# A new order of all steps and fewer idle TensorE products in a single-core hybrid block

## The reference

```
x = x + attention(layernorm(x))   # 16 heads of 8, causal window of 32 plus every 64th key
x = x + ffn(layernorm(x))         # 128 -> 512 -> 512 -> 128, weights +1/-1, relu
x = x + mamba(layernorm(x))       # which itself returns its input plus its output
x = x + ffn(layernorm(x))         # the same ffn again
```

```
h[t] = exp(dt[t] * A) * h[t-1] + (dt[t] * u[t]) * B[t]
y[t] = sum over n of h[t] * C[t]
```

## Time and profile before

| | |
|---|---|
| median of three timed executions | 776.4 us (775.49, 776.4, 776.85) |
| the profiled execution | 773.7 us |
| its span | 771.9 us |
| around the span | 1.8 us |
| mean granted TensorE clock | 0.996 of full speed |

### The profile page before, as it was taken

One profiled execution on the slowest core, in us unless ns is written; L12 is line 12 of the kernel. 1 busy time (PEld: TensorE's weight loads), 2 busy tenths in 40 slices (PEclk: granted clock), 3 DMA queues, 4 the chain that ended last, 5 costly groups with the idle time before them and its releaser, 6 DMA issues. The chain is left out here.

```text
span 771.9 us, 21849 instructions
## 1 busy us (share of the span) xinstructions
PE 710.7 (92%) x8031; PEld 403.9 (52%) x8031; DVE 685.3 (89%) x1138; ACT 640.6 (83%) x1282; POOL 610.4 (79%) x599
## 2 busy tenths in 40 slices
PE   7889999998999989999999999979998999888798
PEld 4676644644555346547555356445464453343356
DVE  6988339989999999999999899999999999899973
ACT  4778688999989999998889999988979866856633
POOL 5013347888998999788898789999999999999960
PEclk9999999999999999999999999999999999999989
DMA  6000014533524161423425171525261525254410
GB/s 211 3 3 2 3 46 152 164 97 107 186 71 138 45 200 63 135 77 107 128 64 183 46 232 58 178 92 174 69 192 46 178 83 178 91 171 144 143 42 28
DMA packets 45003, 83.56 MB, mean 108 GB/s; under 512 B 5081, under 2 KB 5730, under 8 KB 44898
## 3 DMA queue, kind: packets, MB, share of 16 engines
q1 hardware_dynamic: 44898, 82.18, 33.5%
HBM read 71.15 MB, written 11.01 MB: 106 GB/s over the span
## 5 line engine op out<-in xcount | busy, mean ns | idle before, releaser
L1820 POOL TENSOR_TENSOR d<-d,cr 128x1024 f32<-128x1024 f32 x128 | 300.1, 2355 | 17.4 <-DVE d L1315 6.9
L1632 ACT ACTIVATE ps<-dt,An 128x512 f32<-128x512 f32 x252 | 172.2, 696 | 36.7 <-DVE d L1315 36.0
L1315 DVE TENSOR_TENSOR_SCAN d<-ps,hl,d 128x512 f32<-128x512 f32 x128 | 157.2, 1262 | 5.0 <-ACT ps L1632 4.3
L1315 DVE TENSOR_TENSOR_SCAN d<-ps,d 128x512 f32<-128x512 f32 x128 | 149.9, 1205 | 7.2 <-ACT ps L1632 6.9
L886 PE MATMUL ps<-h,w 128*128 128x512 f16 (+1 forms) x512 | 115.8, 379 | 6.6 <-DVE h L1243 6.3
L1303 DVE TENSOR_TENSOR d<-ps,du 128x512 f32<-128x512 f32 x173 | 111.6, 671 | 3.8 <-ACT ps L1615 2.2
L1806 POOL TENSOR_TENSOR d<-du,br 128x512 f32<-128x512 f32 x79 | 99.9, 1276 | 5.7 <-PE ps L981 4.1
L886 PEld LDWEIGHTS ps<-h,w 128*128 128x128 f16 x512 | 48.1, 99 | 76.1 <-DVE h L1243 17.8
L981 PE MATMUL ps<-d,cst 128*32 128x512 f32 x512 | 68.1, 604 | 3.2 <-POOL d L1820 3.2
L897 PEld LDWEIGHTS ps<-w,h 128*128 128x128 f32 x496 | 58.2, 192 | 8.3 <-issue 5.5
L897 PE MATMUL ps<-w,h 128*128 128x128 f32 x496 | 60.6, 277 | 0.8 <-ACT h L1529 0.8
(11 more groups left out here) (186 smaller groups left out, 1373.0 us busy)
## 6 DMA issues: line engine op xcount, KB each, us to landing
cr<-bcd SPq DMA_DIRECT2D x64, 256.0 KB, 3.3
br<-bcd SPq DMA_DIRECT2D x64, 256.0 KB, 3.1
dt<-dtd SPq DMA_DIRECT2D x64, 256.0 KB, 3.9
du<-dud SPq DMA_DIRECT2D x64, 256.0 KB, 3.6
dtd<-sR SPq DMA_DIRECT2D x16, 256.0 KB, 3.0
dud<-sE SPq DMA_DIRECT2D x16, 256.0 KB, 2.3
X<-in_x SPq DMA_DIRECT2D x8, 256.0 KB, 6.4
out<-X SPq DMA_DIRECT2D x3, 512.0 KB, 4.0
```

What stands on the lines that cost most here:

```text
L1315: eng.tensor_tensor_scan(d, banks[u % NG][:, :], d, hl[:, r:r + 1] if m % 2 else 0.0, ALU.mult, ALU.add).then_inc(v_sc, 1)
L1632: eng.activation(banks[u % NG][:, :], src[:, :], ACT.Exp, scale=An[:, g:g + 1]).then_inc(s_da, 1)
L1820: eng.tensor_tensor(d, d, CR[k % NC][:, :].unsqueeze(1).to_broadcast((128, n, 512)), ALU.mult).then_inc(p_cm, n)
```

## The change

Three things change; no instruction outside the idle products is added or removed, and which engine runs a tile's drive stays.

1. All numbers of `PLACES` are new. Compared as orders, 648 of ScalarE's 946 steps stand at another position, 453 of VectorE's 798, 312 of TensorE's 704, 158 of GpSimd's 322 and 230 of the DMA queue's 302. Most move by a few positions; the furthest are `jexp_s(1, 1)` (34 earlier), `aln_p(3, 0)` (40 later), `afar_v(1, 3)` (25 later).
2. `WARM` holds 33 runs with 173 `warm_t` products in place of 32 runs with 207 (the first entry, 8 products of `wake_t`, stays). With numbers over 570,000 stand 106 products in place of 139; of these, with numbers from 690,000 to 730,000, 28 in place of 28.
3. `bdt_t` loses a wait.

```
-    "gate_p": [172166, 214728, 261005, 292325, 372528, 374202, 429085, 457150, 499682, 548281, 574574, 607798, 665247, 680832, 715753],
...
+    "gate_p": [170696, 213613, 247300, 284326, 370996, 373530, 442779, 456599, 514580, 539318, 572679, 603283, 678895, 680122, 721855],
...
-    "silu_s": [100306, 167620, 255442, 322000, 426697, 483530, 573445, 645357],
...
+    "silu_s": [100445, 166698, 254325, 321662, 424921, 483026, 571576, 643475],
...
 WARM = [
-    (8848, 2, 8), (10191, 0, 3), (16231, 2, 8), (21682, 0, 6), (23005, 1, 3), (34876, 3, 2), (111358, 6, 8), (129053, 2, 5),
-    (206279, 7, 4), (263399, 4, 5), (265231, 4, 3), (436700, 7, 8), (457969, 2, 4), (495463, 2, 9), (574181, 7, 4), (585926, 7, 6),
-    (609134, 4, 6), (612224, 4, 4), (614591, 2, 4), (630052, 5, 6), (634479, 5, 14), (647873, 6, 9), (655387, 5, 12), (662679, 5, 15),
-    (679413, 4, 2), (682168, 4, 9), (687207, 5, 12), (690266, 6, 8), (695529, 6, 2), (711634, 7, 9), (714721, 6, 9), (739706, 4, 4), (741039, 5, 4),
+    (8675, 2, 8), (10186, 0, 3), (14787, 3, 4), (20658, 0, 3), (21937, 1, 3), (23263, 2, 3), (29410, 5, 2), (30734, 5, 3), (32013, 6, 1),
+    (34871, 3, 6), (48143, 7, 1), (50796, 3, 4), (127930, 2, 7), (263916, 4, 3), (266254, 6, 5), (269065, 5, 4), (455392, 2, 6),
+    (485725, 6, 6), (497891, 7, 3), (581172, 5, 1), (583181, 5, 4), (609781, 2, 3), (628167, 5, 11), (632542, 5, 14), (645991, 6, 9),
+    (649544, 4, 5), (656822, 5, 11), (679826, 7, 5), (686084, 5, 11), (692945, 5, 8), (710434, 7, 7), (712551, 2, 6), (715831, 6, 7),
+    (738807, 5, 4),
 ]
...
             def bdt_t(u):
 
-                if u > 1:
-                    eng.wait_ge(v_dr, u - 1)
                 bank = bank_of["bdt", u] = turn((s_da, u + 1))
                 eng.wait_ge(v_md, 2)
```

More of the change, by code:

```diff
@@ L179 @@
 PLACES = {
[L180 to L186, removed]
@@ L204 @@
[L204 to L212, removed]
@@ L242 @@
-    "aval_t": [16232, 16680, 28176, 32603, 33051, 34877, 56616, 57645, 68603, 90454, 99525, 129054, 129502, 133411, 192697, 203193, 233946,
-        238553, 269197, 286144, 291188, 292217, 333698, 352184, 407648, 408096, 445309, 458361, 459581, 460610, 530824, 531853],
-    "bdt_t": [117705, 118605, 119505, 122205],
-    "bdu_t": [115905, 116805, 120405, 121305],
-    "bp_s": [115822, 137051, 140835, 148718, 161672, 174139, 182954, 192454, 204593, 216459, 221370, 232392, 241915, 251131, 261356,
[3 rows of a table removed]
@@ new lines @@
+    "akd_v": [13358, 14614],
+    "akp_p": [33632, 131544, 249759, 413738],
+    "aln_p": [5112, 7232, 18702, 31849, 89029, 92109, 302688, 312460],
+    "aln_s": [9910, 10877, 62256, 62733, 208867, 221138, 386243, 391659],
+    "aln_t": [8676, 10187, 59638, 60223, 208087, 219459, 385553, 390164],
+    "aln_v": [17445, 30592, 76776, 77892, 115249, 253963],
+    "an_s": [98206],
+    "ano_s": [6970, 9126, 54224, 55762, 160871, 209958, 345462, 358645],
+    "aown_s": [22436, 26857, 27028, 31845, 32512, 43321, 43492, 43663, 47356, 48945, 49055, 53215, 53325, 53435, 53545, 53853, 63703,
[5 rows of a table added]
@@ new lines @@
+    "aval_t": [14248, 17656, 26739, 32770, 34872, 36196, 54922, 57176, 68409, 87963, 99461, 127931, 128471, 132421, 190672, 201868, 233709,
+        237440, 269878, 286937, 289713, 293784, 332478, 350780, 406009, 406549, 442927, 456717, 457257, 458282, 528542, 529567],
+    "bdt_t": [116927, 117670, 118413, 120084],
+    "bdu_t": [115586, 116050, 119156, 119620],
+    "bp_s": [117276, 136079, 142721, 152540, 160356, 173090, 179797, 192430, 200958, 212784, 220623, 230664, 240788, 247374, 260224,
[3 rows of a table added]
@@ new lines @@
+    "br_d": [109881, 110496, 128339, 131692, 136695, 143337, 153156, 169532, 183312, 189710, 193046, 212586, 221459, 225575, 236557,
[4 rows of a table added]
+    "cr_d": [111111, 114817, 127724, 146096, 149074, 159988, 165577, 182697, 194891, 197926, 211371, 220244, 232513, 235942, 252479,
[4 rows of a table added]
+    "csum_t": [130021, 144891, 154904, 167107, 171324, 181815, 193444, 198042, 213939, 220277, 238073, 240124, 255052, 261913, 273666,
[4 rows of a table added]
+    "decay_s": [117977, 118720, 120109, 121134, 123429, 127182, 127796, 133229, 135465, 137790, 138404, 140046, 141630, 143236, 144145,
[16 rows of a table added]
@@ new lines @@
+    "dt_p": [110785, 127660, 177280, 192547, 262790, 279108, 346136, 379555, 433386, 452715, 495203, 515965, 580534, 604510, 652881,
+        676243],
+    "dt_s": [108931, 124858, 175286, 189613, 260936, 277254, 343631, 376784, 431532, 449226, 492589, 513262, 578664, 600098, 650980,
+        667107],
+    "dt_t": [107776, 123703, 173549, 188458, 259781, 276099, 342329, 375496, 430377, 448071, 491434, 512107, 577509, 598943, 649545,
+        665952],
+    "dt_v": [110225, 126797, 176720, 190907, 262230, 278548, 345441, 378995, 432826, 451831, 493903, 515405, 579958, 602804, 652274,
[6 rows of a table added]
@@ new lines @@
+    "fln_t": [67132, 121699, 218557, 269066, 310425, 364028, 386138, 408496, 505556, 535574, 583182, 603834, 647807, 680719, 708238,
+        737490, 741327],
+    "fln_v": [62915, 114108, 212940, 263337, 278940, 298070, 371453, 399782, 483783, 530118, 572116, 598765, 630902, 644533, 686340,
+        733869, 736538],
+    "flo_v": [68385, 127189, 220115, 271269, 312469, 365456, 387391, 411319, 508509, 537247, 585212, 609040, 651228, 685742, 709693,
+        738323, 742160],
+    "fno_s": [66072, 119334, 216732, 267365, 303006, 361312, 384073, 404403, 498222, 533538, 581481, 602133, 636465, 654379, 706063,
+        736539, 740276],
@@ new lines @@
+    "gate_p": [170696, 213613, 247300, 284326, 370996, 373530, 442779, 456599, 514580, 539318, 572679, 603283, 678895, 680122, 721855],
+    "jexp_s": [54013, 100234, 202087, 221615, 338827, 369718, 505595, 586272],
+    "jmix_p": [56149, 103269, 204953, 252406, 355288, 374989, 519849, 590375],
+    "jout_t": [61014, 109905, 209930, 260834, 368353, 386576, 527556, 596229],
+    "jrec_v": [55545, 102665, 203803, 251135, 354684, 374385, 514947, 588165],
+    "jsub_p": [52635, 90812, 184692, 220171, 333568, 368340, 504217, 579237],
@@ new lines @@
+    "jsum_p": [54395, 100616, 202644, 246223, 351510, 372453, 510840, 586983],
+    "jtr_v": [60252, 109143, 209168, 257607, 362911, 381757, 524541, 594575],
+    "jx_v": [62200, 112150, 211019, 262622, 370215, 388586, 528923, 597570],
+    "lg_v": [732225, 732566],
+    "lm_t": [732710, 734940],
+    "lm_v": [733353, 735583],
+    "lmo_t": [727993, 729023],
+    "lpre_p": [723082],
+    "mln_p": [84830, 146667, 238445, 291543, 408275, 460489, 554584, 628071],
+    "mln_s": [89149, 155591, 243822, 298935, 413580, 468447, 558903, 632390],
@@ new lines @@
+    "mln_t": [89302, 154347, 243006, 298267, 412840, 467694, 559056, 632543],
+    "mln_v": [83535, 145372, 237150, 290248, 406980, 458296, 552903, 626364],
+    "mno_s": [87599, 149511, 241303, 294478, 411044, 463788, 557353, 630840],
+    "mout_t": [214945, 291174, 383573, 459307, 554284, 606961, 681454],
+    "mout_v": [217079, 293657, 386714, 461770, 558941, 609638, 685085],
+    "mu_s": [98817, 99658, 164114, 166122, 251382, 253749, 306787, 319041, 420430, 422135, 474754, 479932, 567565, 571000, 641929, 642899],
@@ new lines @@
+    "mz_t": [94235, 156660, 244891, 300004, 421519, 479071, 562142, 634041],
+    "one_v": [12513],
+    "out_p": [121102, 124997, 131876, 138279, 140942, 143605, 152807, 157261, 159924, 162850, 165534, 174584, 182029, 185989, 188652,
[8 rows of a table added]
+    "out_v": [730181],
+    "scan_v": [118702, 119831, 122154, 123283, 125071, 129111, 134220, 135349, 136478, 138801, 139930, 141771, 142900, 151536, 152665,
[16 rows of a table added]
+    "set_v": [36053, 79008],
+    "silu_s": [100445, 166698, 254325, 321662, 424921, 483026, 571576, 643475],
@@ L432 @@
+    "spr_p": [87829],
+    "store_d": [496482, 710814, 720228, 738135, 747537, 752809],
+    "vz_p": [256],
+    "yev_v": [169522, 208528, 243342, 283534, 327945, 370813, 425843, 452820, 497682, 536607, 570291, 602164, 643893, 679043, 704772],
 }
 WARM = [
[4 rows of a table removed]
[5 rows of a table added]
 ]
```

127 lines of the change are left out of this document (42 added, 85 removed), and 288 rows, old and new, of the table PLACES.

## The result

The kernel after is slower: 778.28 us (median of 12 executions, 774.81 to 780.88) beside 775.48 us for the kernel before (12 executions, 773.49 to 778.86). The ratio is 1.0031 with a 95% interval of 1.0016 to 1.0047, or 2.4 us (the medians themselves lie 2.8 us apart). The forecast was 774.3 us and faster; it started from 776.4 us, the median of the first three executions of before, and its sum of -2.1 us from 775.48 would give 773.4. The profiled execution of after took 776.9 us with a span of 775.1 and a mean granted clock of 0.985 (before: 773.7, 771.9 and 0.996).

What follows compares the result with a forecast made beforehand. No engine was taken to bound the whole span; GpSimd sets the pace from 450 to 742 us. Terms -1.5 - 0.2 - 0.4 = -2.1 us took 776.4 to 774.3 us, range 771.3 to 778.2.

Steps and rivals of the forecast that it cites:

- all other places: Some 1,800 steps moved elsewhere in their queues: taken as 0, bounds -4.1 to +4.1 us.
- rival C: Halves 3, 4 and 6: moved gates make GpSimd reach the softplus too early; 3.8 us lost, 778.1 us, chance 0.12.
- The end of the recurrence: Decays 252 to 255 ahead of four `fl2_s` remove VectorE's and GpSimd's last stops: -1.5 us, range -1.9 to +1.0.
- rival B: At the end the clock falls again and the last `csum_t` wait for `fl2_t`: 775.8 us, chance 0.18.
- The SiLU of half 7 and `bp_s(52)`: Decay 214 and `bp_s(52)` moved ahead on ScalarE: up to 4 us of VectorE's waits go, costed at nothing.
- The wait of `bdt_t`: Wait removed on TensorE ahead of products feeding the first four tiles: -0.2 us, bounds 0 and -0.2.
- Fewer idle products: Idle products taken out or moved earlier on TensorE, most of them filling waits: -0.4 us, bounds 0 and -2.0.
- Rival D: More falls of TensorE's clock between 600 and 700 us, one costing 2.8 us: 777.1 us, chance 0.10.
- Rival A: The order in the middle is better too; GpSimd's stops for scans shrink by 2.7 us: 771.6 us, chance 0.15.

Runs made afterwards that it cites:

- The cuts: Six kernels with before's order and idle products on one side of table number 124,000, 450,000 or 690,000 and after's on the other; ratios to before 0.9994 to 1.0063.
- the two mixed kernels: After's order with before's idle products: 793.28 us, 1.0203 against before; before's order with after's idle products: 790.11 us, 1.0177.

## Why the prediction was wrong

**The failing step: "all other places" at nothing.** The prediction took every place outside those it named as 0 with a width of 4.1 us, and gave no part of it to one side. The cuts put the loss there: the new order and products ahead of 450,000 cost 0.49% by themselves and giving them back takes all of it away, and 2.4 to 2.8 us of it fall to the stretch from 124,000 on, if the head costs as little as the cuts say. The prediction had itself read that a gain must come from that stretch, since GpSimd stands in it; the same reading says that a loss comes from it as easily, and the order of this stretch was not followed step by step.

It had even named one move there, and set it at nothing: with `gate_p(3, 0)` behind the softplus of half 4, GpSimd "can only wait longer". It did: 3.93 us where it had waited 2.49, and the gate's 1.3 us still to do behind it. This is **rival C**, at the first of its three gates, with the sign that the prediction gave for it (over 2.5 us at this line for half 4). GpSimd's whole group of softplus waits grew by 2.0 us, near the size of the loss. And in the kernel with the new order up to 450,000, 1.0 of its 2.0 us come between scan 127 (460.0 us) and scan 129 (464.5), right behind the gate, which runs there at 457.97. The gates of later halves lie behind 450,000, where the new order costs nothing, as the prediction's own reading had it (waits of at most 0.5 us). So the best candidate is one gate, not three. No kernel moved that gate alone, so its price is not shown, nor what does the rest; rival C's 778.1 us lies beside the measured 778.28 by another sum, and that is luck.

Another stop in this stretch looks worse and is not: in after GpSimd stands for 3.20 us at 160 us, where before it stood for 1.46. But the product behind it starts 2.79 us later than in before, and the first scan was already 2.45 us late.

**The end of the recurrence, -1.5: not there in the old order.** The stop of 1.91 us went and the end stayed. The price was taken as the smaller of two waits, VectorE's and GpSimd's; but the chain already ran through TensorE alone, 5.92, 0.99, 3.56, 0.89, 1.84 and 1.98 us, and a wait beside the chain has no price but what slack the chain leaves. In the kernel with this one edit scan 251 is 4.0 us later than in before and scan 252 only 2.0, so VectorE did get its 2.0 us; the last `csum_t` is 3.4 us later all the same. This is the mechanism of rival B (TensorE's time lies ahead of the last `csum_t`), though not as a loss: alone it comes out at 0. The prediction called TensorE thinly used at this end, with 18.3 us of 21.9; that is 83%, and its queue was what set the end. The whole new end, with its products, was worth 2.5 us behind the new order (0.32%, above), so 0 holds for the order of before; why it differs was not looked into.

**The SiLU of half 7 and `bp_s(52)`, 0: right.** With both edits the ratio is 1.0001, without them 1.0007, which fits the reason given: GpSimd is the pace there and had no stop.

**The wait of `bdt_t`, -0.2:** too small to see beside first scans that differ by up to 3 us between profiles of one head, and not tried by itself.

**Fewer idle products, -0.4: wrong sign, and not one sum.** Only their own time was counted. Three of the runs dropped held the clock up in the old order and were worth 4.2 us there. In the new order putting them back costs 6 us more than after. So the price of a product can't be carried from one order to the other. One way for it to cost was seen: a product that waits holds up what stands behind it in TensorE's queue.

**Rival D, more falls between 600 and 700 us: seen, and not the cause.** The falls came (clock 0.90 from 665 to 700 us), but the kernel with the old order up to 450,000 has the falls at 597, 676 and 689 us as well and is as fast as before, and products at four places, after which the profile has three falls in place of seven, gave nothing. The first reading of the result was that they cost what was lost; it fell with that run and with the cuts. Rival A, a better middle, has the place right and the sign wrong; behind 450,000 the new order may gain: 0.5 us by one side of the cut, 1.4 by the other, neither beyond its interval.

**The forecast's own range.** The prediction gives 772.8 to 775.6 us as what the bounds of the small terms leave. They leave more: the lower bounds, -1.9, -0.2 and -2.0, give 772.3 from 776.4, and the upper, +1.0, 0 and 0, give 777.4.

## What to carry to other kernels

Before pricing a stop that a reordering removes, look whether it is in the chain that ended last; the one of 1.91 us was not, and was worth nothing. The profile follows that chain back only to 712 us, so for the stops of 2.60 and 1.7 us, worth nothing either, the reading was which engine never stands. A move that can only make the pacing engine wait longer has a price, not a zero. Where a new order moves hundreds of steps, cut it by stages from both sides early: the six cut kernels located what edits of single suspects did not. Then try the suspects inside the stretch they leave: that step is missing here. Idle products belong to the order they were placed for, and have to be placed anew, by measurement, with each order.

## What was not expected of the hardware

The granted clock differs between executions of one binary, and the time goes with it. The 126 executions of before that were taken alongside the experiments fall into a few levels of mean clock:

| mean granted clock | executions | mean time, us |
|---|---|---|
| 0.998 | 1 | 774.46 |
| 0.996 | 39 | 774.66 |
| 0.993 | 40 | 775.63 |
| 0.991 | 34 | 776.86 |
| 0.989 | 3 | 777.62 |
| 0.987 | 9 | 779.31 |

With two levels, a mean clock c means 2(1 - c) of the time at half clock: 6 us at 0.996, 20 us at 0.987. A straight line through the 126 gives 772.6 us plus 0.31 us (0.04 either way) for each of these, so in a kernel with four busy engines a microsecond at half clock went with a third of one. The Trainium skill ("TensorE: Matmul & The Clock Gate", Part 1) says that the moment of a change of the clock moves from run to run. No run here shows the moment within one kernel's executions, but one case comes near: the profile of before has no fall up to 700 us, and the five profiles of other kernels with its steps and products up to 450,000 all have one between 50 and 54 us. The profiled execution of before, at 0.996, was among its fastest, which made the profile look nearer to a kernel without falls than its median is. And the third is no price that can be moved to another kernel: the kernel with four places filled had 11 us at half clock, after 23 (means over 12 executions each), with the same time.

The second was how much a misplaced run of idle products costs: with about the same number of them, 207 and 173, the two mixed kernels came out 1.8 and 2.0% above before, more than the 1.5% that leaving nearly all of them out costs.
